# Moving gate weights out of the router and into the token sums of a fused attention and mixture-of-experts kernel

## The chip, the cores and the metric

One core of one Trainium2 chip runs the whole block as one program. The metric is the device time of an execution in microseconds (us). Smaller is better.

## The reference

Inputs are x (4 x 1024 tokens of 256), a context of 4 x 154 rows of 192, a key mask and two gates. With layernorm LN:

```
x = x + tanh(g_xattn) * Attention(LN(x), ctx, mask)   # 8 heads of 64
x = x + tanh(g_ffn)   * FFN(LN(x))
FFN(h): scores = sigmoid(h @ gate_w.T)                 # 32 experts in 8 groups of 4
        sc = scores + e_bias; keep the 4 groups with the largest sum of their top 2
        pick the top 6 of what is left; w = scores there / (their sum) * 2.5
        out = sum over the 6 of w * relu(h @ up_e.T)^2 @ down_e.T     # inner 128
            + relu(h @ up_sh.T)^2 @ down_sh.T                        # inner 512
```

## The kernel before

The 4096 tokens are 32 tiles of 128 (the partitions). Every engine runs a program written out by hand; semaphores order them. Helpers are called in loops over a slot T or a pair p, and the order of the calls in a slot is the engine's order.

**Maps.** PE makes keys and values of the context in 16 groups through a ring of seven PSUM banks; ACT saves the even groups, VectorE (DVE) the odd ones. In ACT's program the tanh of the gates stands ahead of all saves, and behind the loads of context and constants that ACT issues (L489 to L499). In DVE's, the constants (L701 to L708) stand ahead of all saves. SP loads weights, x and a transposed x.

**Attention.** In slot T of 35, PE does the scores of tile T (L1167), transposes the probabilities of tile T-2 (L1200), queries of T+2 (L1113), head outputs of T-2 (L1213) and the output projection of T-3 (L1223). DVE takes maxima (L751), inverts sums, normalises every other pair of tiles, adds the residual and takes its statistics. ACT makes exponentials and copies. The router works on blocks of four tiles, spread over slots: statistics to normed tiles in `norm_out` (T % 4 == 2), transposes and logits on PE (T % 4 == 3), `router_groups` and `router_select` (T % 4 == 0), `ranks` on PE and `router_slots` on DVE (T % 4 == 1). `router_slots` also makes a one-hot array `hot` and `picked`, its product with the scores (L913, L916); the weights are summed and scaled in instructions threaded through the next `norm_out` (L785 to L807).

**Rows.** POOL scatters each normed tile six times, once for each pick, to `routed_rows` in DRAM, at the place that the rank gives in its expert's region (L443). A row holds 256 values, six place keys (`R_ID`), six weights (`R_W`), six target rows (`R_TO`) and two more, 276 in all. Six scatters are issued in a slot from T = 11 on, each behind a wait on the other engines' progress (`slot_step`); the last 54 follow without such waits.

**Tables.** Counts of each expert give 224 tiles of 128 rows. SP writes a padding tile at each expert's end (32 DMAs of 138 KB), then loads rows.

**Expert pairs.** For p in 0 to 111: SP loads two tiles of rows to a ring of six pairs; PE does `expert_down` (L1428) of p-2, `expert_up` (L1413) of p and transposes (L1401) of p+2; ACT saves transposes, copies up weights (L640) and scales and saves the output of even pairs (L651); DVE does `relu_square` (L1038, L1040), `pick_rows` for two pairs (weights and target rows, L1024 to L1033), and scales and saves odd pairs (L1049). POOL scatters the outputs to `token_parts` (L479), into eight buffers in turn. Row tiles from pair 14 on wait for all of the scatters of `routed_rows`. In 28 of the pairs, PE also does a step of the shared expert (`SHARED_STEP`; L1299 up, L1309 down). From p = 51 on ACT loads the six parts of a token tile (768 KB) every 2.2 pairs (`PART_LOAD`), and DVE adds them in three steps in the three pairs from p + 3 (L1057; L1059, L1060; L1062).

**End.** Four shared down products and adds in turn on one bank, then the last four token tiles: two parts added by DVE, four by PE with an identity (L1455), the sum by DVE (L1093).

## Time and profile before

| | |
|---|---|
| median of 3 runs | 759.53 us (757.47 to 766.26) |
| profiled execution | 762.32 us, its span 760.5 us |
| mean granted TensorE clock | 0.989 |
| busy: PE, DVE, ACT, POOL | 705.1 (93%), 518.9 (68%), 454.1 (60%), 469.1 us (62%) |
| DRAM | 144.74 MB in 78238 packets, mean 190 GB/s |

Busy is the time in which an engine has an instruction in work; waits and drains do not count. A row of the timeline has the start in us from the span's start, the duration, engine, line, operation, tiles and shapes, and in brackets the idle time ahead of it with what ended it.

### The profile page before, as it was taken

Reading aid. Unit: us, or ns where it says so; the run is one execution under the profiler, and the core shown is the slowest. Engines: PE = TensorE matmul, PEld = TensorE weight load, DVE = VectorE, ACT = ScalarE, POOL = GpSimd, SP = SyncE. Lnnn points to the kernel's source line nnn. Section 1 sums busy time; section 2 is a strip of 40 time slices with the busy share of each in tenths; the row PEclk is TensorE's granted clock in tenths of the full one; section 3 lists DMA queues with packets and bytes.
Section 4 is the critical chain, followed back from the end, with each engine's and each line's share of the span. In section 5 each row is a group of like instructions: output and inputs, shape, how many; then the busy total and the mean of one; then the engine's idle time right before and its main releaser. Section 6 shows DMA issues by size and latency. Waiting matters only on the chain.

```text
span 760.5 us, 17775 instructions
## 1 busy us (share of the span) xinstructions
PE 705.1 (93%) x5416; PEld 600.7 (79%) x5416; DVE 518.9 (68%) x1783; ACT 454.1 (60%) x1299; POOL 469.1 (62%) x478
## 2 busy tenths in 40 slices
PE   7979898999999999989998999999998999999968
PEld 7768797888888888775674898988897788888756
DVE  0757578787878787876461556555567788888783
ACT  0257576778787878773515556566655666566620
POOL 1235442466666666577777477777775777777671
PEclk9999999999999999999999999999999999999998
DMA  9970000135222222354759866656689999999854
GB/s 311 376 227 1 1 3 1 54 105 190 89 96 93 91 91 91 110 189 158 275 176 303 227 212 194 207 169 185 211 262 290 327 325 351 316 369 315 261 208 153
DMA packets 78238, 144.74 MB, mean 190 GB/s; under 512 B 13750, under 2 KB 60097, under 8 KB 77120
## 3 DMA queue, kind: packets, MB, share of 16 engines
q1 hardware_dynamic: 51472, 67.46, 28.7%
q0 software_dynamic: 19968, 52.34, 18.8%
q10 hardware_dynamic: 6704, 23.80, 9.4%
q8 instruction: 45, 0.74, 0.4%
q14 instruction: 49, 0.40, 0.2%
HBM read 78.00 MB, written 69.73 MB: 194 GB/s over the span
## 4 chain that ended last, share of the span: by engine, by line
PE 46%; DVE 17%; DMA 9%; POOL 7%; issue 7%; ACT 6%; DVEq 6%; SPq 2%; ACTq 1%; POOLq 0%
PE ps L1428 8%; PE ps L1413 7%; POOL routed_rows L443 7%; DMA mid<-routed_rows 7%; PE ps L1401 4%; PE ps L1223 4%; PE ps L1213 4%; PE ps L1309 4%; ACT att L529 3%; PE ps L1167 3%; PE ps L1113 2%; PE ps L1200 2%; DMA gate_w<-in_gate_t 2%; DVEq L1076 2%; PE ps L1299 2%
## 5 line engine op out<-in xcount | busy, mean ns | idle before, releaser
L443 POOL DMA_INDIRECT routed_rows<-x_n,slots x120 | 119.9, 999 | 68.1 <-issue 31.6
L479 POOL DMA_INDIRECT token_parts<-hid,place x112 | 114.6, 1024 | 50.6 <-issue 26.2
L1428 PE MATMUL ps<-big,att 128*128 x448 | 118.8, 388 | 6.7 <-DVE picked L1049 3.2
L627 ACT ACTIVATE att<-ps 128x512 f32<-128x512 f32 x96 | 57.3, 597 | 97.4 <-PE ps L1401 96.2
L1413 PEld LDWEIGHTS ps<-att 128*128 128x128 f32 x768 | 100.8, 192 | 5.0
L1413 PE MATMUL ps<-att 128*128 128x128 f32 x768 | 101.2, 275 | 0.0
L1428 PEld LDWEIGHTS ps<-big,att 128*128 128x128 f32 x448 | 78.4, 190 | 27.0 <-issue 20.2
L529 ACT ACTIVATE att<-ps,nmax,rstd 128x154 f32<-128x154 f32 x176 | 82.0, 494 | 13.4 <-DVE nmax L756 13.2
L1213 PE MATMUL ps<-att,big 128*64 128x128 f32 x1024 | 70.3, 280 | 16.0 <-ACT att L546 11.3
L640 ACT ACTIVATE att<-big 128x256 f32 x224 | 80.1, 408 | 1.9 <-issue 1.2
L1213 PEld LDWEIGHTS ps<-att,big 128*64 128x64 f32 x1024 | 59.6, 138 | 23.5 <-ACT att L546 13.8
L1401 PE MATMUL ps<-cst,mid 128*128 128x128 f32 x448 | 67.9, 274 | 9.6 <-DMA mid<-routed_rows 9.4
L546 ACT ACTIVATE att<-ps 128x512 f32<-128x512 f32 (+1 forms) x96 | 48.4, 551 | 32.2 <-PE ps L1200 32.2
L751 DVE TENSOR_REDUCE nmax<-ps 128x3 f32<-128x462 f32 (+1 forms) x96 | 52.2, 572 | 20.0 <-PE ps L1167 20.0
L443 POOL DMA_INDIRECT routed_rows<-big,slots x48 | 49.6, 1032 | 22.0 <-issue 11.4
L1113 PE MATMUL ps<-big,hid 128*128 128x128 f32 x512 | 62.6, 275 | 0.0
L1401 PEld LDWEIGHTS ps<-cst,mid 128*128 128x128 f32 x448 | 52.1, 141 | 12.5 <-DMA mid<-routed_rows 9.9
L1038 DVE TENSOR_SCALAR hot<-ps 128x256 f32<-128x256 f32 x56 | 23.8, 425 | 54.6 <-PE ps L1401 53.0
L1223 PE MATMUL ps<-hid,big 128*128 128x256 f32 x256 | 61.0, 381 | 0.0
L1113 PEld LDWEIGHTS ps<-big,hid 128*128 128x128 f32 x512 | 59.7, 192 | 0.3 <-issue 0.3
L1223 PEld LDWEIGHTS ps<-hid,big 128*128 128x128 f32 x256 | 46.2, 190 | 5.8 <-issue 0.5
L529 ACT ACTIVATE big<-ps,nmax,rstd 128x154 f32<-128x154 f32 x80 | 37.3, 496 | 5.3 <-DVE nmax L756 5.3
(252 smaller groups left out, 1450.4 us busy)
## 6 DMA issues: line engine op xcount, KB each, us to landing
mid<-routed_rows SPq DMA_DIRECT2D x224, 138.0 KB
big<-token_parts ACTq DMA_DIRECT2D x19, 768.0 KB, 7.2
x_n<-token_parts ACTq DMA_DIRECT2D x9, 768.0 KB
routed_rows<-pad_row SPq DMA_DIRECT2D x1, 4416.0 KB
routed_rows<-pad_row SPq DMA_DIRECT2D x32, 138.0 KB
x_all<-in_x SPq DMA_DIRECT2D x4, 1024.0 KB, 12.9
big<-in_x_t SPq DMA_DIRECT2D x4, 1024.0 KB, 15.6
big<-in_w_moe SPq DMA_DIRECT2D x2, 2048.0 KB, 8.8
```

The source lines that it names most:

```text
L443: nc.gpsimd.indirect_dma_start(rows, bass.IndirectOffsetOnAxis(ap=slots[:, t, k:k + 1], axis=0), normed(t), None).then_inc(s_sca[t // TB % ...
L479: nc.gpsimd.indirect_dma_start(parts, bass.IndirectOffsetOnAxis(ap=place[:, p // 2 % 8, p % 2 * 2 + j:p % 2 * 2 + j + 1], axis=0), y_sb[p ...
L529: ins = A.activation(prob[T % 3][:, h * JP:h * JP + J], ps[:, q, i * J:(i + 1) * J], ACT.Exp, bias=nmax[:, T % 2, h:h + 1], scale=rstd1[:, ...
L627: A.activation(xt(p), ps[:, p % 2, :], ACT.Copy).then_inc(s_xts, 1)
L640: ins = A.activation(w_up[p % 2][:, j, :], w_exp[:, bass.ds(e, 1), 0:256].rearrange("p a n -> p (a n)"), ACT.Copy)
L751: V.tensor_reduce(nmax[:, T % 2, h:h + n], ps[:, q, 0:n * J].rearrange("p (a j) -> p a j", a=n), op=ALU.max, axis=AX_X, negate=True)
L1113: ins = M(ps[:, 6, m * P:(m + 1) * P], wq[:, c, m * P:(m + 1) * P], xt_in[:, T, c, :], start=c == 0, stop=c == KC - 1, skip_group_check=True)
L1213: ins = M(ps[h % 2 * DH:(h % 2 + 1) * DH, 7, h // 2 * P:(h // 2 + 1) * P], v_all[b][:, at:at + DH], prob_t[:, c * P:(c + 1) * P], start=c ...
L1223: ins = M(ps[:, 7, 0:D], att_t[:, m * P:(m + 1) * P], wo[:, m, :], start=m == 0, stop=m == MC - 1, skip_group_check=True)
L1401: ins = nc.tensor.transpose(ps[:, p % 2, j * 256 + c * P:j * 256 + (c + 1) * P], ring[:, p % 6, j, c * P:(c + 1) * P], ident)
L1413: ins = M(ps[:, 2 + p % 2, j * P:(j + 1) * P], w_up[p % 2][:, j, c * P:(c + 1) * P], xt(p)[:, j * 256 + c * P:j * 256 + (c + 1) * P], star ...
L1428: ins = M(ps[:, 6 + p % 2, j * D:(j + 1) * D], h_t[:, p % 2, j * P:(j + 1) * P], w_exp[:, bass.ds(e, 1), 256:512].rearrange("p a n -> p (a ...
```

## The change

1. Rows no longer carry weights (270 values). SP stores the router's scores of each block to DRAM and loads them all back ahead of row tile 14. In pairs 16 to 47 DVE finds each pick's expert from its place (a region is now 9 x 512 rows), marks it, picks the score and norms the weights to `w_tok`. `add_parts` becomes six multiply-adds. ACT and DVE save expert outputs unscaled; the wait for `pick_rows` goes from ACT's save to POOL's scatter.
2. Attention: `router_select` is split; the second part runs in T % 4 == 1 behind maxima and residual. `ranks` runs behind the head outputs, `router_slots` in T % 4 == 2 ahead of statistics and `norm_out`.
3. POOL's scatters start at slot 10, place k = 3; a memset (`pause`) follows each of the 51 behind the slots.
4. Start: SP loads the context first; tanh and constants move between the saves.
5. End: the last block's shared up steps move out of the pairs to behind them, on banks 0 to 3; down products alternate between two banks; the last tiles' parts are summed by DVE alone.

```diff
-REGION = N_TOK + P
+REGION = 9 << 9
+PAUSE = 320
-R_ID, R_W, R_TO, R_BASE, ROW = D, D + TOPK, D + 2 * TOPK, D + 3 * TOPK, D + 3 * TOPK + 2
+R_ID, R_TO, R_BASE, ROW = D, D + TOPK, D + 2 * TOPK, D + 2 * TOPK + 2
+WEIGH = {16 + 2 * i: 2 * i for i in range(NT // 2)}
+NORM_T = 8
-LATE = [(i, s) for i in range(FULL, NBLK) for s in range(8) if i >= GAP or s >= 4][:-TB]
+LATE = [(i, s) for i in range(FULL, NBLK) for s in range(8) if i >= GAP or s >= 4][:-2 * TB]
...
+            load_ctx(0)
             sp.dma_start(wk, w_k).then_inc(s_wk, 16)
             sp.dma_start(wv, w_v).then_inc(s_wv, 16)
+            load_ctx(2)
+            sp.dma_start(wq, w_q).then_inc(s_wq, 16)
             load_x(0)
-            sp.dma_start(wq, w_q).then_inc(s_wq, 16)
...
+            def store_scores(b):
+                sp.wait_ge(s_score, b + 1)
+                sp.dma_start(scores[:, b * TB * NE:(b + 1) * TB * NE], score[:].rearrange("p t e -> p (t e)")).then_inc(s_sst, 16)
...
                     sp.wait_ge(s_zf, 16 * (NE + 1))
+                    sp.wait_ge(s_sst, 16 * NBLK)
+                    sp.dma_start(old_rows[:, 0:NT * NE], scores).then_inc(s_sld, 16)
                 load_rows(p)
...
+            def pause():
+                if paused[0]:
+                    pool.wait_ge(s_pause, paused[0])
+                else:
+                    pool.wait_ge(s_xb, NT)
+                paused[0] += 1
+                nc.gpsimd.memset(bias_o[:].bitcast(BF16)[:, 0:PAUSE], 0.0).then_inc(s_pause, 1)
...
-            for T in range(11, NT + 2):
+            for T in range(10, NT + 2):
                 for k in range(TOPK):
                     slot_step(T, k)
-                    scatter((T - 11) * TOPK + k)
-            for i in range((NT + 2 - 11) * TOPK, NT * TOPK):
+                    if (T - 10) * TOPK + k >= 3:
+                        scatter((T - 10) * TOPK + k - 3)
+            for i in range((NT + 2 - 10) * TOPK - 3, NT * TOPK):
                 scatter(i)
+                pause()
...
                 pool.wait_ge(s_ey[p % 2], p // 2 + 1)
+                pool.wait_ge(s_pick, p // 2 + 1)
...
-            act.wait_ge(s_const, 16 * 6)
-            A.activation(tanh_g[:], gates[:], ACT.Tanh).then_inc(s_tanh, 1)
-            act.drain()
...
-                if g == 8:
+                if g == 6:
+                    act.wait_ge(s_const, 16 * 6)
+                    A.activation(tanh_g[:], gates[:], ACT.Tanh).then_inc(s_tanh, 1)
+                    act.drain()
+                if g == 12:
                     act.wait_ge(s_wo, 16)
...
-                act.wait_ge(s_pick, p // 2 + 1)
-                for j in range(2):
-                    ins = A.activation(y_sb[p % 8][:, j * D:(j + 1) * D], ps[:, 6, j * D:(j + 1) * D], ACT.Copy,
-                                       scale=pair_w[:, p // 2 % 8, j, 0:1])
-                ins.then_inc(s_ey[0], 1)
+                A.activation(y_sb[p % 8], ps[:, 6, :], ACT.Copy).then_inc(s_ey[0], 1)
...
-                if g == 3:
+                if g == 5:
                     stats(0)
                     stats(2)
                     norm_in_scale(0, 4)
+                if g == 7:
+                    constants()
...
+                if T % 4 == 1 and T >= 9:
+                    residual_add(T - 3)
+                    router_select()
...
-                    if T % 4 or T < 8:
+                    if T % 4 > 1 or T < 8:
                         residual_add(T - 3)
+                    if T % 4 == 2 and T >= 10:
+                        router_slots((T - 10) // 4)
                     residual_stats(T - 3)
-                if T % 4 == 1 and T >= 9:
-                    router_slots((T - 9) // 4)
...
-                    router_select((T - 8) // 4)
+                    router_top_groups()
...
+            def mark_experts(t):
+                V.tensor_tensor(hot, w_tok[:, t:t + 2, :].unsqueeze(3).broadcast_to([P, 2, TOPK, NE]),
+                                iota_e.unsqueeze(1).unsqueeze(1).broadcast_to([P, 2, TOPK, NE]), ALU.is_equal)
+            def pick_scores(t):
+                dve.drain()
+                V.tensor_tensor(hot, hot, score_t[:, t:t + 2, :].unsqueeze(2).broadcast_to([P, 2, TOPK, NE]), ALU.mult)
+                dve.drain()
+                V.tensor_reduce(w_tok[:, t:t + 2, :], hot, op=ALU.add, axis=AX_X)
+            def add_weighted(t, g, k):
+                return V.scalar_tensor_tensor(x_all[:, t, :], g[:, k, :], w_tok[:, t, k:k + 1], x_all[:, t, :], ALU.mult, ALU.add)
             def add_parts(t, step):
                 g = parts_sb[t % 3]
                 if step == 0:
                     dve.wait_ge(s_pl[t % 3], 16 * (t // 3 + 1))
-                    V.tensor_tensor(g[:, 0:3, :], g[:, 0:3, :], g[:, 3:6, :], ALU.add)
...
+                add_weighted(t, g, 2 * step)
+                dve.drain()
+                ins = add_weighted(t, g, 2 * step + 1)
...
+                for k in range(TOPK):
+                    if k == TOPK - 1 and t < NT - 1:
+                        add_late(t)
+                        dve.drain()
+                    ins = add_weighted(t, sums[:, t - NT + N_LAST, :, :], k)
+                    dve.drain()
+                ins.then_inc(s_fin, 1)
...
-                if T % 4 == 1 and T >= 9:
-                    ranks((T - 9) // 4)
                 if 2 <= T < NT + 2:
                     probs_t(T - 2, 1)
...
                     heads_out(T - 2)
+                if T % 4 == 1 and T >= 9:
+                    ranks((T - 9) // 4)
...
+            for s in range(4):
+                if s in (0, 2):
+                    pe.wait_ge((s_xts, s_eht)[s // 2], N_PAIRS)
+                up_late(LAST, s)
             for t in range(NT - TB, NT):
                 down_late(t)
-            for t in range(N_LAST):
-                pe.wait_ge(s_pl2[t], 16)
-                for k in range(2, TOPK):
-                    ins = M(ps[:, t, 0:D], ident, sums[:, t, k, :], start=k == 2, stop=k == TOPK - 1)
-                ins.then_inc(s_pp, 1)
```

## Rows read from the trace of the kernel before

**Rows 1.** Timeline of the head.
```profile
7.44 4.39 PE L1125 MATMUL ps<-mid,hid 128*128 128x308 f32 x16 [1.38 <-DMA mid<-in_ctx_t]
...
20.03 0.20 ACT L499 ACTIVATE tanh_g<-gates 128x2 f32<-128x2 f32 x1 [11.79 <-DMA gate_w<-in_gate_t]
...
20.80 2.89 PE L1134 MATMUL ps<-hid,mid 128*128 128x128 f32 x16 [3.61 <-ACT big L517]
...
41.02 0.50 PE L1157 MATMUL ps<-mask_bf,ones_bf 64*128 64x308 bf16 x3
```

**Rows 2.** Timeline of PE, slots 24 to 26.
```profile
262.51 1.33 PE L1167 MATMUL ps<-big 64*128 64x154 f32 x16
...
279.83 1.31 PE L1213 MATMUL ps<-att,big 128*64 128x128 f32 x18 [1.37 <-ACT att L546]
...
281.28 1.33 PE L1167 MATMUL ps<-big 64*128 64x154 f32 x16
```

**Rows 3.** Timeline of DVE: norm_out 0, maxima 25, norm_out 5, places of block 6.
```profile
97.71 0.17 DVE L782 TENSOR_SCALAR nwt<-mv 128x4 f32<-128x4 f32 x1
...
100.66 0.74 DVE L822 TENSOR_SCALAR x_n<-x_all,mv,rstd 128x256 f32<-128x256 f32 x2
...
274.56 0.58 DVE L751 TENSOR_REDUCE nmax<-ps 128x3 f32<-128x462 f32 x1
...
286.39 0.17 DVE L782 TENSOR_SCALAR nwt<-mv 128x4 f32<-128x4 f32 x1
...
290.92 1.50 DVE L822 TENSOR_SCALAR big<-x_all,mv,rstd 128x256 f32<-128x256 f32 x4
...
350.60 0.26 DVE L888 TENSOR_TENSOR key<-ps,cst 128x128 f32<-128x128 f32 x1
...
352.47 0.95 DVE L913 TENSOR_TENSOR hot<-key,best 128x768 f32<-128x768 f32 x1
```

**Rows 4.** Timeline of PE, pairs 14, 32 and 36.
```profile
449.71 0.60 PE L1401 MATMUL ps<-cst,mid 128*128 128x128 f32 x4
...
504.81 1.05 PE L1413 MATMUL ps<-att 128*128 128x128 f32 x8
...
515.61 1.05 PE L1413 MATMUL ps<-att 128*128 128x128 f32 x8
```

**Rows 5.** DVE's waits (total, times, longest) in 423:546, then in 563.56:719.06.
```profile
DVE hot L1038 <- PE ps L1401: 27.8, 23, 2.4
DVE x_n L1038 <- PE ps L1401: 16.2, 23, 1.6
...
DVE hot L1038 <- PE ps L1401: 6.5, 8, 1.8
DVE x_n L1038 <- PE ps L1401: 4.4, 5, 2.4
```

**Rows 6.** One window: length, busy of PE, PEld, DVE, ACT, POOL; clock, DMA, GB/s.
```profile
563.56:719.06 155.50, 146.74 (x930) 126.82 (x928) 128.97 (x364) 93.16 (x227) 111.62 (x106) 1.00 0.95 319
```

**Rows 7.** Timeline of POOL: a memset, first and last scatter behind the slots.
```profile
3.35 0.38 POOL L420 MEMSET run<- 128x352 bf16 x1
...
354.56 0.96 POOL L443 DMA_INDIRECT routed_rows<-big,slots  x1 [0.30 <-issue]
...
421.88 0.96 POOL L443 DMA_INDIRECT routed_rows<-att,slots  x1 [0.30 <-issue]
```

**Rows 8.** Timeline of DVE: old sums of a token tile, a multiply-add.
```profile
645.43 0.96 DVE L1057 TENSOR_TENSOR big<-big 128x768 f32<-128x768 f32 x1
...
647.90 0.41 DVE L1059 TENSOR_TENSOR big<-big 128x256 f32<-128x256 f32 x1
...
650.53 0.48 DVE L832 SCALAR_TENSOR_TENSOR x_all<-ps,tanh_g,x_all 128x256 f32<-128x256 f32 x1
```

**Rows 9.** Timeline of the end: a down product of PE, DVE's last add.
```profile
740.29 3.78 PE L1309 MATMUL ps<-w_shared,hid 128*128 128x256 f32 x8 [4.13 <-DVE x_all L832]
...
757.94 0.42 DVE L1093 TENSOR_TENSOR x_all<-ps,x_all 128x256 f32<-128x256 f32 x1 [0.47 <-PE ps L1455]
```

More of the change, by code:

```diff
@@ L66 @@
 DONE = [-(-((TOPK * P * t + NE * (P - 1)) // P) // 2) for t in SEG_END[:-1]]
+WEIGH = {16 + 2 * i: 2 * i for i in range(NT // 2)}
+NORM_T = 8
+assert N_TOK + P <= REGION == 9 << 9 and max(WEIGH) < 56 and all(9 * e * 57 >> 9 == (9 * e + 8) * 57 >> 9 == e for e in range(NE))
 assert (TOPK * P * EARLY - NE * (P - 1)) // P >= 2 * EARLY_PAIRS
@@ L306, in x2t_bank, with down_bank, up_bank @@
             return 5 if j == 0 else 6 if b < NBLK - 1 else 4
+        def down_bank(t):
+            return 4 if t >= NT - TB and t % 2 else 5
+        def up_bank(i, s):
+            return 4 if i < LAST else s
         def xt(p):
@@ L459, in slot_step @@
                     pool.wait_ge(s_pt, 3 * T - 3)
-            for T in range(11):
-                if T < 10:
-                    normalise(T)
+            for T in range(10):
+                normalise(T)
                 if T < 8:
@@ L486, in _ @@
             A = nc.scalar
-            for b in range(0, NB, 2):
-                for c in range(2):
-                    act.dma_start(ctx_w[:, c, b:b + 2, P:P + J],
-                                  ctx_t[:, c, b * J:(b + 2) * J].rearrange("p (b j) -> p b j", b=2)).then_inc(s_ctx[b // 2], 16)
             act.dma_start(gates[:, 0:1], g_xattn.partition_broadcast(P)).then_inc(s_const, 16)
@@ L699, in newton, with constants @@
                     dve.drain()
[L701 to L708 removed]
+            def constants():
+                dve.wait_ge(s_const, 16 * 6)
+                dve.wait_ge(s_tanh, 1)
+                dve.wait_ge(s_mrow, 16)
+                V.tensor_scalar(mask_bf[:].rearrange("p b j -> p (b j)"), mask_u8, -1.0, MASKED / DH, ALU.add, ALU.mult).then_inc(s_mask, 1)
+                V.tensor_copy(tri_bf[:], cst[:, C_TRI:C_TRI + P])
+                V.tensor_scalar(bias_o[:], bias_o[:], tanh_g[:, 0:1], None, ALU.mult)
+                dve.wait_ge(s_clr, 1)
+                V.memset(pad_row[:, R_BASE:R_BASE + 1], 1.0).then_inc(s_ready, 1)
             def stats(t):
@@ L779, in norm_out @@
                 a, half, tmp = [nwt[:, i, 0:TB] for i in range(3)]
-                r, w = normed_blk(max(b - 1, 0)), weight[:]
                 dve.drain()
@@ L899, in router_slots @@
                 dve.drain()
-                V.tensor_copy(normed_blk(b)[:, :, R_ID:R_ID + TOPK], best[:, :, 0:TOPK])
-                V.tensor_scalar(slots[:, TB * b:TB * b + TB, :], best[:, :, 0:TOPK], -1.0, None, ALU.add)
                 if TB * b + 3 in SEG_END:
@@ new lines, in norm_weights @@
+            def norm_weights(t):
+                w = w_tok[:, t:t + NORM_T, :]
+                dve.drain()
+                V.tensor_reduce(total[:], w, op=ALU.add, axis=AX_X)
+                dve.drain()
+                V.tensor_scalar(total[:], total[:], 1e-20, None, ALU.add)
+                dve.drain()
+                V.reciprocal(total[:], total[:])
+                dve.drain()
+                V.tensor_scalar(total[:], total[:], tanh_g[:, 1:2], ROUTED_SCALE, ALU.mult, ALU.mult)
+                dve.drain()
+                ins = V.tensor_tensor(w, w, total[:].unsqueeze(2).broadcast_to([P, NORM_T, TOPK]), ALU.mult)
+                if t + NORM_T == NT:
+                    ins.then_inc(s_wt, 1)
@@ L1056, in add_parts @@
                     dve.wait_ge(s_pl[t % 3], 16 * (t // 3 + 1))
-                    V.tensor_tensor(g[:, 0:3, :], g[:, 0:3, :], g[:, 3:6, :], ALU.add)
-                elif step == 1:
-                    V.tensor_tensor(g[:, 0, :], g[:, 0, :], g[:, 1, :], ALU.add)
-                    V.tensor_tensor(x_all[:, t, :], x_all[:, t, :], g[:, 2, :], ALU.add)
-                else:
-                    V.tensor_tensor(x_all[:, t, :], x_all[:, t, :], g[:, 0, :], ALU.add).then_inc(s_fin, 1)
+                add_weighted(t, g, 2 * step)
+                dve.drain()
+                ins = add_weighted(t, g, 2 * step + 1)
+                if step == 2:
+                    ins.then_inc(s_fin, 1)
             for p in range(N_PAIRS + 2):
@@ L1081, in _ @@
                         dve.drain()
-            for t in range(NT - TB, NT):
-                add_late(t)
-            dve.drain()
             for t in range(NT - N_LAST, NT):
-                g = sums[:, t - NT + N_LAST, :, :]
+                if t == NT - 1:
+                    add_late(t)
+                    dve.drain()
                 dve.wait_ge(s_pl2[t - NT + N_LAST], 16)
-                V.tensor_tensor(g[:, 0, :], g[:, 0, :], g[:, 1, :], ALU.add)
-                dve.drain()
-                V.tensor_tensor(x_all[:, t, :], x_all[:, t, :], g[:, 0, :], ALU.add)
-                dve.drain()
-                dve.wait_ge(s_pp, t - NT + N_LAST + 1)
-                V.tensor_tensor(x_all[:, t, :], ps[:, t % 4, 0:D], x_all[:, t, :], ALU.add).then_inc(s_fin, 1)
+                for k in range(TOPK):
+                    if k == TOPK - 1 and t < NT - 1:
+                        add_late(t)
+                        dve.drain()
+                    ins = add_weighted(t, sums[:, t - NT + N_LAST, :, :], k)
+                    dve.drain()
+                ins.then_inc(s_fin, 1)
         @block.tensor
```

144 lines of the change are left out of this document (72 added, 72 removed).

## The prediction, made before the result was known

> **What bounds the kernel now.** I read the stages first, then in each one the wait that ends last. Of the span of 760.5 us, the first 41.5 us set up, an attention loop of 32 slots ends near 356, shared work and tables run to 414, 112 pairs of expert tiles to 734, and the end takes the rest. In all of them TensorE is nearly always busy, but what breaks its row differs.
>
> Head: PE waits 3.61 us for a copy that ACT makes at 20.3, because ACT's first instruction, the tanh, waits for the last constant, to 20.03 [rows 1].
>
> Attention: slots 24 and 25 together take 18.8 us (262.51 to 281.28). PE's own work is 8.4 in each, and 0.3 for the ranks in slot 25, which holds a wait of 1.37 at the head outputs, for a copy by ACT [rows 2]. So slot 25 takes 10.4. Its scores were ready near 272.2, but VectorE took their first maximum at 274.56 [rows 3], behind the expert selection. ACT's exponentials, and the copies behind them, start late by those 2.3 us.
>
> Expert pairs: four pairs take 10.80 us while PE alone is the limit (504.81 to 515.61) [rows 4]: 2.19 a pair, 1.7 for a shared step that is in one of the four, some 0.3 for loading registers. From about pair 54, when finished tokens are also summed, VectorE has little left: it waited 44.0 us in 423 to 546, and only 10.9 in the 155.5 us from the up product of pair 54 to that of pair 107 [rows 5], though PE idles there too for want of rows. DMA is busy 95% of that stretch [rows 6].
>
> **The change, part by part**, in us of the profiled execution (762.3 with 1.8 outside its span; the median of the runs, 759.5, stands 2.8 lower, so I add the sum to that).
>
> *Head.* ACT's context loads go to SP's queue ahead of the rest, and tanh moves behind the save of map group 4. PE then has no reason for the 3.61 wait; VectorE's constants move behind group 7, so its first copies, held back as well, come early: the 16 matmuls behind the wait span 2.89, about 1.1 over their work, and the next groups stall again, together some 1.5 (an estimate). The start at 7.44 waited 1.38 for the context [rows 1]; it is now first on its queue but the key weights come third, bounds 0 and 1.38, I take 0.5. Tile loads follow later on SP; I estimate 13 to 15 us against their use in VectorE's group 5. Sum -5.5, bounds -3 to -6.5. If x were late, its statistics would only delay group 7, which PE needs 12 us later.
>
> *Attention.* Selection is cut: top groups stay in the slot T % 4 == 0, the 2.5 us from the comparison to the selected mask move behind the maxima of the next slot, ranks behind that slot's head outputs. VectorE's work in T % 4 == 0, from the first maximum about 10 us, falls by 2.5 and below 8.4, so the maxima come when the scores do. The slot of 10.4 should take 8.7: 1.65 each, six slots (9 to 29): -9.9. Against it: places move into T % 4 == 2, ahead of the normalisation. From key to places is 1.87 us (350.60 to 352.47), about 1.95 with the copy of target rows; the weights that were threaded through norm_out go, 4.53 us with them (286.39 to 290.92) and 2.95 without (97.71 to 100.66) [rows 3]. Net 0.35 later for the normed tiles, which PE's next transposes already wait for: six times, +2.1. Slot 33 gains a wait for the mask, +0.5. Sum -7.3; bounds -4 and -10. Slots then sit at PE's own work, so nothing beyond this is to be had. The removed one-hot product, multiply and sum (three of 0.95 a block) save nothing more, since they lay beside PE. Storing scores costs eight small DMAs on SP, whose waits all come before the weight loads behind them are due: 0.
>
> *Tables to the first pair.* The places of the last block are free of weights, but PE is still in its shared products when they come. 0.
>
> *Pauses.* Scatters begin three earlier, so 51 instead of 54 are left when the slots end: at 1.27 each from 354.56, they would end at 419.3 rather than 422.8. But each of the 51 is now followed by a memset of 320 bf16 on POOL. The nearest row is the memset of 352 bf16, 0.38 us [rows 7]. The gap of 0.30 ahead of every scatter may hide most of it (0.05), or be paid twice (0.65). I take 0.38: POOL ends at 438.7. Queued behind are the output scatters, some 9 us later than now, and on SP the wait for all scatters before row tile 14, then the 512 KB of scores. PE transposes pair 14 at 449.71 [rows 4]; landing (about 3), issue and the loads (about 6.5) end at 448. It fits by 1.5 us. Up to 0.41 a pause costs nothing, 0.65 costs 12. POOL, 9 us later, is just inside the eight output buffers: +1.
>
> *Early pairs, weights.* VectorE makes the token weights in pairs 16 to 47: per two tiles a comparison, a product and a sum of 384 elements. 768 take 0.95 [rows 3], so 384 about 0.55, 1.63 with two drains; times 16 is 26.1; four norms of 1.35, 5.4; the expert numbers, 1.6; less 16 times 0.06 for a smaller pick: 32.1. Idle was 44.0 in 46 pairs, 30.6 in these 32. VectorE is full: +1.5. With POOL's 1: +2.5, bounds -2 (rows sooner in emptier queues) and +14 (pauses exposed).
>
> *Late pairs.* A tile's sum was one add of 768 at 0.96 and three of 256 at 0.41 to 0.42, with drains and overlap 2.37. It becomes six multiply-adds of 256 with a per-partition scalar, each behind a drain. The trace has that form only from PSUM, 0.48 [rows 8]; adds cost the same from either memory, so six times (0.48 + 0.07) is 3.3, +0.93. If the scalar were free, six times 0.49 gives +0.6. VectorE worked 155.5 - 11.7 = 143.8 us in the stretch (its waits for PE are 10.9, two others 0.8). 24 tiles add 22.3, the smaller pick takes 1.6: 164.5, and with 1 us of leftover idle the stretch takes 165.5: +10. With a free scalar 158: +3. This also eats what four shared up products (6.9 us of PE), moved behind the loop, would have given.
>
> This is the point where the Trainium skill speaks against the change. The rows show three times the elements at 0.96 against 0.41, so 0.27 us of the smaller cost follow the elements and 0.15 come with each instruction. The Trainium skill (VectorE: DVE Perf Modes, the section on the TRN2 errata) says that operations on SBUF pay a fixed latency per instruction and wants tiles of 512 elements or more; its formula for fp32 adds, (N + 151) / 0.96, gives an estimate of 2.54 us for six against 2.23 for the old four, +0.3 a tile before drains and scalar. By that alone the stretch would be about 3 us shorter than mine. The trace agrees with the formula to 2%.
>
> *End.* Before, the last tiles went down, add, down on one bank, one down product taking 3.78, twice its usual 1.9, from 740.29 to the last add at 757.94 [rows 9]. Now PE does four ups after pair 111 (6.9), the squares end 1.3 later, and down products alternate banks. VectorE finishes its queue 2 us later than it did (four dearer tiles less idle), then does seven operations of 0.55 for each of four tiles: 15.4 where it was 18.7 (the last pair's sums ended at 739.7). PE holds the first back 0.7. Sum -0.7, bounds -3 and +5 (downs at half clock).
>
> Sum: -5.5 - 7.3 + 2.5 + 10 - 0.7 = -1.0. That is 758.5.
>
> **Rivals.** *Late pairs are not VectorE's (faster).* For: VectorE had 10.9 us to spare, PE loses 6.9 us of work, and the price of the multiply-add is not seen from SBUF. Against: of those 10.9 most fall where PE itself waited for rows. With +1 to +3 for the stretch, the head and attention stay whole: 749.5.
>
> *Pauses exposed (slower).* In POOL's tail, at a pause of 0.65 a scatter, SP's wait before tile 14 holds every later row: +12, so 770. It decides from 0.41. For: gaps between scatters are never under 0.30, so another instruction may add its own. Against: that memset of 0.38 was itself followed by the next after 0.32.
>
> *The end at half clock.* PE idles more beside a full VectorE and meets the last downs at 3.8 instead of 1.9: +5, 763.
>
> *The stall moves.* The change does not do what it says: places and normalisation fill T % 4 == 2 (about 9.5 us for 8.4), and the stall returns one slot later. Then attention gives 1 instead of 7.3: 765.
>
> **How the numbers follow.** Forecast 0.42 (own range 752 to 765), late pairs cheap 0.32, pauses 0.14, half clock 0.05, stall moves 0.07. A measurement of this kernel cannot tell 1% from no change. Faster by over 1% (under 751.9) takes nearly all of the second and a little of the first: 0.36. Slower by over 1% (over 767.1) takes pauses, half of the last and the forecast's upper tail: 0.22. Within: 0.42. The range leaves one in ten outside at each end: 746 to 771.
>
> **What would show it.** Head: first scores near 35.5 instead of 41.02. Attention: T % 4 == 1 slots at 8.7, and T % 4 == 3 slots 0.3 longer. Pauses: spacing of the last 51 scatters 1.65, and no PE wait for rows at pair 14. Late pairs: VectorE without waits, 3.1 us a pair, PE idle. The multiply-add at 0.48. I am wrong if PE's cadence past pair 54 stays 2.9 or less, or if tile 14 is waited for.

## The result and the profile after

The changed kernel takes 769.8 us (median of 20 runs, 766.95 to 774.77) where the kernel before takes 760.8 on the same chip (756.01 to 767.39): a ratio of 1.0121, 95% interval 1.0100 to 1.0142. It is slower, by 1.2%. The prediction was 758.5. Medians and ratios, here and in the experiments, leave out the few executions that ran far longer than the rest (1005.5 us once in experiment 1, 1404.0 once in experiment 2). The profiled execution took 769.17 us, its span 767.4, at a mean granted clock of 0.982.

Cut at the same events, the two spans differ like this (starts of the scores of slots 0 and 3, of the up products of pairs 0, 54 and 107, and the span's end; all from TensorE's timeline):

| stretch | before | after | difference | predicted |
|---|---|---|---|---|
| to the first scores | 41.23 | 36.17 | -5.06 | -5.5 (head) |
| slots 0 to 2 | 21.02 | 23.99 | +2.97 | 0 |
| slot 3 to pair 0 | 354.05 | 346.48 | -7.57 | -7.3 |
| pairs 0 to 54 | 147.26 | 146.44 | -0.82 | +2.5 |
| pairs 54 to 107 | 155.50 | 170.94 | +15.44 | +10 |
| pair 107 to the end | 41.46 | 43.36 | +1.90 | -0.7 |
| span | 760.52 | 767.38 | +6.86 | -1.0 |

The stretch of pairs 54 to 107, one window as in [rows 6]: length, busy time of PE, PEld, DVE, ACT and POOL, clock, DMA share and rate.

```profile
553.08:724.02 170.94, 143.72 (x913) 126.28 (x912) 145.15 (x411) 83.39 (x196) 109.24 (x109) 0.98 0.90 292
```

Beside [rows 6] DVE has 16 us more to do in 47 more instructions, PE 3 less, and DMA is less busy. What PE waits for in that window (total, times, longest), and what DVE does (busy us, mean ns, idle ahead of it):

```profile
PE ps L1492 <- DVE spare L1065: 9.6, 6, 1.9
PE ps L1492 <- DVE hid L1065: 7.5, 7, 1.9
PE ps L1492 <- DVE att L1057: 3.7, 8, 0.6
PE ps L1492 <- DVE big L1065: 3.2, 2, 2.1
PE ps L1465 <- DMA mid<-routed_rows: 2.9, 1, 2.9
```

```profile
L1105 DVE SCALAR_TENSOR_TENSOR x_all<-big,w_tok,x_all 128x256 f32<-128x256 f32 x96 | 46.3, 482 | 4.8
L1105 DVE SCALAR_TENSOR_TENSOR x_all<-x_n,w_tok,x_all 128x256 f32<-128x256 f32 x46 | 22.1, 481 | 2.3
```

The down product (L1492) waits for VectorE's copy of an output out of its bank (L1065) or for its square (L1057), 24.0 us in all; in the kernel before its waits for VectorE are 0.9, and those for rows 6.3. What keeps VectorE so long stands in the second fence: 142 multiply-adds of 0.48 us. How they follow each other, in VectorE's timeline of two pairs:

```profile
599.71 1.03 DVE L1105 SCALAR_TENSOR_TENSOR x_all<-x_n,w_tok,x_all 128x256 f32<-128x256 f32 x2
600.83 1.04 DVE L1105 SCALAR_TENSOR_TENSOR x_all<-big,w_tok,x_all 128x256 f32<-128x256 f32 x2
601.95 0.42 DVE L1055 TENSOR_SCALAR spare<-ps 128x256 f32<-128x256 f32 x1
602.46 0.42 DVE L1057 SCALAR_TENSOR_TENSOR att<-ps,spare 128x256 f32<-128x256 f32 x1
...
603.63 0.16 DVE L1050 TENSOR_TENSOR place<-pair_to,to_spill 128x4 uint32<-128x4 f32 x1
603.71 1.04 DVE L1105 SCALAR_TENSOR_TENSOR x_all<-big,w_tok,x_all 128x256 f32<-128x256 f32 x2
604.82 0.42 DVE L1055 TENSOR_SCALAR x_n<-ps 128x256 f32<-128x256 f32 x1
```

There is no gap: a step of two, each behind a drain, takes 1.12 to 1.14 us from start to start (600.83 less 599.71, 601.95 less 600.83), three steps 3.4 a tile where the prediction reads 2.37 for the old sum.

The attention loop, against [rows 2] and [rows 3]: PE's slots 24 to 26, and VectorE's maximum of slot 25.

```profile
254.86 1.33 PE L1228 MATMUL ps<-big 64*128 64x154 f32 x16
...
263.23 1.33 PE L1228 MATMUL ps<-big,x_n 64*128 64x154 f32 x16
...
269.25 2.22 PE L1274 MATMUL ps<-att,big 128*64 128x128 f32 x32
271.40 0.23 PE L1321 MATMUL ps<-sel,tri_bf 128*128 128x128 bf16 x1
...
271.92 1.33 PE L1228 MATMUL ps<-big 64*128 64x154 f32 x16
```

```profile
264.62 0.64 DVE L798 TENSOR_REDUCE nmax<-ps 128x3 f32<-128x462 f32 x1 [0.49 <-PE ps L1228]
```

Slot 25 takes 8.69 us and has no wait at the head outputs (L1274); the maximum now waits for the scores, not they for it. One slot in four (T % 4 == 3) pays for it. PE's timeline in slot 19:

```profile
210.08 1.39 PE L1299 MATMUL ps<-cst,x_n 128*128 128x128 f32 x8 [0.99 <-DVE x_n L853]
```

The transposes of the normed tiles wait 0.99 us for the normalisation.

The pauses, in POOL's timeline against [rows 7]:

```profile
343.71 0.96 POOL L489 DMA_INDIRECT routed_rows<-big,slots  x1 [0.30 <-issue]
344.67 0.38 POOL L483 MEMSET bias_o<- 128x320 bf16 x1
345.22 0.97 POOL L489 DMA_INDIRECT routed_rows<-big,slots  x1 [0.17 <-issue]
346.18 0.39 POOL L483 MEMSET bias_o<- 128x320 bf16 x1
```

A scatter with its pause takes 1.51 us (345.22 less 343.71), 0.25 more than the 1.26 without. The last scatter ends at 421.64, before the up product of pair 14 at 444.09, and nobody waits for it.

The end, VectorE's last tiles, against [rows 9]:

```profile
747.66 3.87 DVE L1105 SCALAR_TENSOR_TENSOR x_all<-big,w_tok,x_all 128x256 f32<-128x256 f32 x7
752.32 0.48 DVE L863 SCALAR_TENSOR_TENSOR x_all<-ps,tanh_g,x_all 128x256 f32<-128x256 f32 x1 [0.79 <-PE ps L1373]
...
761.94 3.28 DVE L1105 SCALAR_TENSOR_TENSOR x_all<-big,w_tok,x_all 128x256 f32<-128x256 f32 x6
```

From 747.66 to 765.22 there is one gap of 0.79: this is one chain of drained multiply-adds.

### The profile page after: what moved, and what is told of

The parts are those of the page before. It is cut to its first block, busy times and chain, and to the rows that moved or that the text cites. A ratio compares the mean times of both kernels' runs of the same rounds, so it can differ in the third digit from the quotient of the medians.

```text
span 767.4 us, 17935 instructions
## 1 busy us (share of the span) xinstructions
PE 699.0 (91%) x5384; PEld 599.4 (78%) x5384; DVE 547.4 (71%) x1859; ACT 441.6 (58%) x1243; POOL 484.1 (63%) x529
## 4 chain that ended last, share of the span: by engine, by line
PE 51%; DVE 24%; DVEq 11%; issue 7%; ACT 3%; DMA 2%; SPq 2%; POOL 0%; ACTq 0%; POOLq 0%
DVE x_all L1105 8%; PE ps L1274 6%; PE ps L1284 6%; PE ps L1174 5%; DVEq L1112 4%; PE ps L1339 4%; PE ps L1492 4%; PE ps L1228 4%; PE ps L1261 3%; PE ps L1477 3%; PE ps L1351 3%; DMA mid<-routed_rows 2%; PE ps L1195 2%; PE ps L1465 2%; PE ps L1373 2%
## 5 line engine op out<-in xcount | busy, mean ns | idle before, releaser
L1492 PE MATMUL ps<-big,att 128*128 x448 | 121.8, 395 | 30.6 <-DVE spare L1065 13.1
L527 POOL DMA_INDIRECT token_parts<-hid,place x112 | 112.7, 1006 | 46.5 <-issue 25.4
L1492 PEld LDWEIGHTS ps<-big,att 128*128 128x128 f32 x448 | 79.2, 193 | 50.6 <-issue 43.4
L1274 PE MATMUL ps<-att,big 128*64 128x128 f32 x1024 | 69.6, 281 | 6.3 <-DVE x_all L816 4.1
L527 POOL DMA_INDIRECT token_parts<-spare,place x56 | 56.5, 1010 | 29.7 <-issue 14.5
L1105 DVE SCALAR_TENSOR_TENSOR x_all<-big,w_tok,x_all 128x256 f32<-128x256 f32 x138 | 66.6, 483 | 7.8
L1274 PEld LDWEIGHTS ps<-att,big 128*64 128x64 f32 x1024 | 60.1, 138 | 12.8 <-DVE x_all L816 5.5
L489 POOL DMA_INDIRECT routed_rows<-big,slots x48 | 48.3, 1005 | 23.1 <-issue 14.6
```

Source lines behind the costliest of these rows:

```text
L489: nc.gpsimd.indirect_dma_start(rows, bass.IndirectOffsetOnAxis(ap=slots[:, t, k:k + 1], axis=0), normed(t), None).then_inc(s_sca[t // TB % ...
L527: nc.gpsimd.indirect_dma_start(parts, bass.IndirectOffsetOnAxis(ap=place[:, p // 2 % 8, p % 2 * 2 + j:p % 2 * 2 + j + 1], axis=0), y_sb[p ...
L1105: return V.scalar_tensor_tensor(x_all[:, t, :], g[:, k, :], w_tok[:, t, k:k + 1], x_all[:, t, :], ALU.mult, ALU.add)
L1274: ins = M(ps[h % 2 * DH:(h % 2 + 1) * DH, 7, h // 2 * P:(h // 2 + 1) * P], v_all[b][:, at:at + DH], prob_t[:, c * P:(c + 1) * P], start=c ...
L1492: ins = M(ps[:, 6 + p % 2, j * D:(j + 1) * D], h_t[:, p % 2, j * P:(j + 1) * P], w_exp[:, bass.ds(e, 1), 256:512].rearrange("p a n -> p (a ...
```

## The experiments

These numbers of each kernel are compared throughout. "Idle" is the sum of the gaps of over 0.12 us between VectorE's rows in the stretch from pair 54 to 107, "work" the stretch less that (instructions and their drains). Each ratio is to runs of the kernel before that were made beside that experiment, on the same chip; their medians were 762.2 to 762.8 us (760.8 beside the changed kernel), so medians of different rows can differ by some 2 us for that alone, and kernels are compared by ratio. The other columns come from one trace each.

| kernel | median, us | ratio to before, 95% | pair 0 starts | pairs 0 to 54 | 54 to 107: length, idle, work | 107 to end |
|---|---|---|---|---|---|---|
| before | 760.8 | 1 | 416.3 | 147.3 | 155.5, 12.0, 143.5 | 41.5 |
| changed | 769.8 | 1.0121 (1.0100 to 1.0142) | 406.6 | 146.4 | 170.9, 5.1, 165.8 | 43.4 |
| 1: no pauses | 775.9 | 1.0204 (1.0096 to 1.0313) | 407.4 | 147.5 | 168.7, 2.5, 166.2 | 44.8 |
| 2: plain sums | 750.6 | 0.9873 (0.9828 to 0.9918) | 406.4 | 148.1 | 149.8, 7.4, 142.3 | 41.9 |
| 3: late ups in pairs | 768.6 | 1.0109 (1.0079 to 1.0140) | 406.7 | 147.6 | 171.2, 5.4, 165.9 | 42.6 |
| 4: head only | 758.4 | 0.9957 (0.9928 to 0.9985) | 413.4 | 147.8 | 154.3, 10.8, 143.4 | 40.8 |
| 5: mixed sums | 754.5 | 0.9917 (0.9878 to 0.9956) | 405.2 | 148.1 | 155.6, 7.1, 148.5 | 42.0 |
| 6: ranks split | 767.6 | 1.0061 (1.0034 to 1.0088) | 402.2 | 148.3 | 170.3, 4.3, 166.0 | 44.8 |
| 7: no token weights | 768.9 | 1.0077 (1.0041 to 1.0112) | 409.7 | 145.6 | 168.4, 2.0, 166.4 | 45.0 |
| 8: mixed, split, end | 749.0 | 0.9812 (0.9773 to 0.9852) | 401.9 | 148.8 | 154.8, 6.4, 148.5 | 41.0 |
| 9: before, half parts | 756.5 | 0.9925 (0.9891 to 0.9959) | 419.1 | 148.0 | 148.3, 4.3, 144.0 | 39.6 |
| 10: changed, half parts | 772.2 | 1.0136 (1.0070 to 1.0202) | 409.9 | 148.9 | 168.7, 2.5, 166.2 | 43.7 |

Five kernels have the changed kernel's code in the late pairs: the changed one and experiments 1, 3 (but for the up products), 6 and 7. They took 168.4 to 171.2 us with 2.0 to 5.4 of it idle. What an experiment moves there by less than that says little.

**1. No pauses.** The changed kernel without them:

```diff
             for i in range((NT + 2 - 10) * TOPK - 3, NT * TOPK):
                 scatter(i)
-                pause()
```

> The changed kernel without the 141 clears of GpSimd between the tail scatters. Theory (VectorE's multiply-adds in the late pairs made the loss): the tail ends some 35 us sooner, nobody waits for it, and the time stays within 2 us of the changed kernel, 768 to 771. Rival (the pauses are exposed): the time falls by 6 us or more, to 764 or less, and the first 30 pairs get shorter.

The scatters ended at 408.9 instead of 421.6, 13 us sooner and not 35 (51 pauses stand there, not the 141 that the expectation counts), and the pairs to 54 were 1.1 us longer, not shorter. The median of three runs, 775.9, is above the 768 to 771 that was expected, and its interval is wide; it holds the changed kernel's ratio. Nothing speaks for a price of the pauses: the rival falls.

**2. Plain sums.** The 24 tiles that are summed in the pairs are added as before the change, so their gate weights are left out:

```diff
-                add_weighted(t, g, 2 * step)
-                dve.drain()
-                ins = add_weighted(t, g, 2 * step + 1)
...
+                    V.tensor_tensor(g[:, 0:3, :], g[:, 0:3, :], g[:, 3:6, :], ALU.add)
+                elif step == 1:
+                    V.tensor_tensor(g[:, 0, :], g[:, 0, :], g[:, 1, :], ALU.add)
+                    V.tensor_tensor(x_all[:, t, :], x_all[:, t, :], g[:, 2, :], ALU.add)
+                else:
+                    V.tensor_tensor(x_all[:, t, :], x_all[:, t, :], g[:, 0, :], ALU.add).then_inc(s_fin, 1)
```

> The changed kernel with the sums of the 24 tiles that go in the pairs written as before, without the gate weights (their part of the output is therefore left unweighted); all else as changed. Theory: VectorE gets 24 x 1.05 = 25 us of work back, TensorE or the output slots bound the late pairs, which fall from 171 to 152 to 158 us, and the time is 752 to 758, below the kernel before. Rival (the late pairs are long because of transfers or GpSimd's scatters, which now run in another order): the late pairs stay at 165 or more and the time at 764 or more.

```profile
554.49:704.24 149.75, 139.48 (x914) 123.87 (x912) 127.75 (x364) 83.55 (x196) 111.59 (x107) 1.00 0.97 331
```

The late pairs fell by 21.2 us, to 149.8, and the kernel to 750.6. VectorE's work fell by 23.5 us (25 expected). This one edit turns a loss of 1.2% into a gain of 1.3%; transfers and scatters were left as they are, and DMA moved more per us than in any other run. The multiply-adds, with the drain behind each, are the cause of the loss. (TensorE's granted clock is 0.98 of full speed in the changed kernel's stretch and 1.00 in this one. That is 3.4 us at most, 2% of 171, of the 21.2.)

**3. Late up products in the pairs.** The last block's four shared up products go back among the pairs (the four calls behind the loop, on PE and ACT, and their banks are taken out as well):

```diff
-LATE = [(i, s) for i in range(FULL, NBLK) for s in range(8) if i >= GAP or s >= 4][:-2 * TB]
+LATE = [(i, s) for i in range(FULL, NBLK) for s in range(8) if i >= GAP or s >= 4][:-TB]
```

> The changed kernel with the last block's four shared up products back in the pairs, as before the change, instead of behind them. Theory (VectorE bounds the pairs and the end alike): TensorE has the room, the late pairs grow by 0 to 2 us, the end loses 0.8 to 2, the time stays within 2 us of 770. Rival (the up products behind the pairs are what made the end 1.9 us longer, and they were worth nothing in the pairs): the time falls by 3 us or more, to 767 or less.

6.9 us of TensorE's work came back into the stretch and it grew by 0.3; the end lost 0.8, less than the ends of kernels with the same code there differ (43.4 to 45.0). The ratio hardly differs from the changed kernel's. TensorE has room there, as the theory says, and moving that work out of the pairs shows no gain beside a full VectorE.

**4. The head alone**, on the kernel before: the context first on SP's queue, ahead of the key weights, tile loads behind the query weights, tanh at group 6, and on VectorE:

```diff
-                if g == 3:
+                if g == 5:
                     stats(0)
...
+                if g == 7:
+                    constants()
```

> The kernel before, with nothing of the change but its first loads, the tanh, the constants and the first statistics where the change has them. Theory: the first scores start 5 us sooner (36.2 for 41.2) and all that follows moves with them, so the time falls by 4 to 5.5 us, to 755 to 757 where the kernel before has 760.8. Rival (the work that the head gives up fills slots 1 and 2, which were 3.0 us longer in the changed kernel): the first pair starts only 2 to 3 us sooner and the time falls by 2 to 3.

Scores started at 36.0, 5.2 sooner, but slot 3 only 3.6 sooner and pair 0 only 2.9; the median fell by 4.0 us against the runs beside it, and the ratio is 0.43% under 1 (3.3 us, 1.1 to 5.5). By its size that is between theory and rival, and the interval holds both. The rival's reason can be tested on the traces. Here are slots 0 to 2, one window each as in [rows 6], with the old head in the kernel before and in experiment 9, then with the new one in experiments 3 and 4 and in the changed kernel:

```profile
41.23:62.25 21.02, 14.42 (x151) 12.39 (x149) 14.09 (x52) 14.29 (x55) 8.60 (x8) 1.00 0.50 155
42.33:64.97 22.64, 17.04 (x151) 14.82 (x149) 14.35 (x54) 14.24 (x55) 8.59 (x8) 0.85 0.40 126
36.27:57.28 21.01, 14.41 (x151) 12.38 (x148) 14.07 (x52) 14.28 (x55) 8.60 (x8) 1.00 0.92 246
36.03:58.67 22.64, 17.13 (x151) 14.91 (x148) 14.36 (x54) 14.24 (x55) 8.59 (x8) 0.85 0.77 237
36.17:60.16 23.99, 18.81 (x151) 16.43 (x149) 14.63 (x54) 14.23 (x55) 8.59 (x8) 0.79 0.77 218
```

The number third from the end is TensorE's mean granted clock; it has two levels, 2.4 GHz (1.00) and 1.2 GHz (0.50). At full clock these slots take 21.0 us with either head, and at 0.85 22.64 with either; VectorE is busy for 14.1 to 14.6 us and ACT for 14.2 to 14.3 in all five. The changed kernel's extra 3.0 us came with some 10 us at 1.2 GHz, and not with work that the head gave up: the rival's reason is wrong. Just ahead of the first fall, in 39.30 to 42.70, TensorE was busy for 0.78 us; in experiment 3 it was busy for as little in the same stretch, and its clock stayed full. The lower clock shows in these slots in seven of the ten traces with the new head and in one of the two with the old, too few to say that the head brings it on.

**5. Mixed sums.** The same multiply-adds in the same order on each tile. In even pairs the first of a step stands among the operations that pick the places, in odd pairs all first ones stand ahead of one drain and all second ones behind it:

```diff
                 V.tensor_reduce(pair_to[:], pick[:], op=ALU.add, axis=AX_X)
+                for t, step in firsts:
+                    add_half(t, step, 0)
                 dve.drain()
                 V.tensor_tensor(place[:, q % 8, :], pair_to[:], to_spill[:], ALU.add).then_inc(s_pick, 1)
+                for t, step in seconds:
+                    add_half(t, step, 1)
```

> The changed kernel with the same multiply-adds, but the first of each step is put among the operations that pick the places (even pairs) or beside that of another tile, and the drains that stood behind each of the two are left to those that stand there anyway. Theory (VectorE's time, of it a good part the drains, sets the late pairs): each step falls from 1.14 us to 0.75 to 0.85, 72 steps by 0.3 to 0.4 = 21 to 28 us of VectorE, the late pairs go from 171 to 153 to 160 us and the time to 752 to 760. Rival (the multiply-adds themselves at 0.48 cost the time, drains lie beside them): the late pairs fall by less than 5 us and the time stays at 765 or more.

VectorE's timeline, to be held against the one of the changed kernel above:

```profile
600.57 1.83 DVE L1109 SCALAR_TENSOR_TENSOR x_all<-big,w_tok,x_all 128x256 f32<-128x256 f32 x4
603.13 0.42 DVE L1059 TENSOR_SCALAR spare<-ps 128x256 f32<-128x256 f32 x1 [0.74 <-PE ps L1476]
```

```profile
553.23:708.82 155.59, 142.94 (x913) 126.76 (x912) 136.47 (x411) 82.60 (x194) 108.24 (x107) 0.98 0.95 317
```

Two steps take 1.83 us from start to end where they took 2.16 (599.71 to 601.87), and then VectorE waits for TensorE. That had waited 1.80 us for rows until 598.43, and from 599.7 to 603.1 its granted clock was half (eight up products took 1.92 us there, 1.05 elsewhere). Busy time fell by 8.7 us with the same 411 instructions, because two that overlap count once; work fell by 17.3 us, about 0.24 a step, less than the 0.3 to 0.4 that was expected. The late pairs and the time came out inside the forecast, 155.6 and 754.5: with the weights in the sums, and faster than before.

**6. Ranks split.** One operation of the ranks' work stays ahead of the normalisation, since it frees the bank; the rest goes behind it:

```diff
                     if T % 4 == 2 and T >= 10:
-                        router_slots((T - 10) // 4)
+                        read_ranks((T - 10) // 4)
                     residual_stats(T - 3)
...
                     norm_out((T - 6) // 4)
+                if T % 4 == 2 and T >= 10:
+                    router_slots((T - 10) // 4)
```

> The changed kernel, with only the one operation that reads the ranks out of the bank ahead of the normalisation in every fourth slot, and the rest of the ranks' work behind it. Theory (the normed tiles come late in slots T mod 4 = 3, since the whole of the ranks' work now stands ahead of them): each of the six slots falls by 0.4 to 0.9 us and the first pair starts 2 to 5 us sooner, the time is 765 to 768. Rival (the next wait stands right behind it): those slots fall by less than 0.3 each and the time stays.

PE's waits between slots 11 and 31 of the changed kernel, then of this one (total, times, longest):

```profile
PE ps L1299 <- DVE x_n L853: 2.5, 3, 1.0
PE ps L1274 <- ACT att L590: 1.6, 1, 1.6
PE ps L1299 <- DVE big L853: 1.4, 2, 0.9
```

```profile
PE ps L1279 <- ACT att L590: 1.6, 1, 1.6
```

The wait is gone, and slots 11, 15, 19, 23 and 27 fell from 55.5 us to 50.0, 1.1 each: more than the wait itself and more than expected. Slot 31 starts 8.3 us sooner than in the changed kernel, 1.8 of which are there at slot 3 already. Pair 0 starts only 4.5 sooner:

```profile
399.30 1.09 PE L1470 MATMUL ps<-cst,mid 128*128 128x128 f32 x4 [5.50 <-DMA mid<-routed_rows]
```

PE waits 5.50 us for the first rows, where the changed kernel has 1.88. So 3.6 us of the gain end there, and TensorE's granted clock is half from 396.5 to 406.8, where the changed kernel has it full; the first 16 pairs take 1.7 us longer. The ratio falls from 1.0121 to 1.0061, some 4.6 us, and the two intervals do not overlap.

**7. No token weights.** A constant stands in place of each token's gate weights, and the work that makes them is left out:

```diff
-                if p == min(WEIGH):
-                    experts_of_tokens()
...
+                    V.memset(w_tok[:], 0.25).then_inc(s_wt, 1)
```

> The changed kernel with the pairs' work on the tokens' weights left out: VectorE writes one constant in their place, so that the sums carry a wrong weight; all else as changed. Theory (that work lies almost wholly in VectorE's idle time): pairs 16 to 48 fall from 89.05 us by 0.5 to 1.5 and the time by as much. Rival (it costs what it takes, some 30 us of VectorE's work over 40 pairs, and delays what follows): pairs 16 to 54 fall by 4 us or more.

VectorE's waits in pairs 16 to 48, of the changed kernel and of this one:

```profile
DVE spare L1055 <- PE ps L1465: 1.7, 3, 0.7
```

```profile
DVE spare L1055 <- PE ps L1460: 18.6, 16, 2.4
DVE x_n L1055 <- PE ps L1460: 10.2, 14, 1.7
```

28.8 us of waits become 1.7 by that work, and the 32 pairs go from 86.58 to 89.05. It is 27 us of work for 2.5 of time. That is between theory and rival. Of the total no change is shown: the ratio, 1.0077, is 0.44% lower, and the intervals overlap.

**8. All three.** Mixed sums, split ranks, and at the end each tile's seven operations start three behind those of the tile ahead of it, two or three tiles between one pair of drains:

```diff
+            for slot in range(3 * (N_LAST - 1) + TOPK + 1):
+                for i in range(N_LAST):
+                    t, k = NT - N_LAST + i, slot - 3 * i
...
+                dve.drain()
```

> The changed kernel with the mixed sums of the run before (754.5), the ranks' work behind the normalisation, and the last four tiles' sums run two at a time, three steps apart, instead of one after the other. Theory: 754.5, less 2 to 4 for the slots, less 1 to 3 for the end, 748 to 752, which is faster than either kernel by over 1%. Rival (the end is bound by the last tile's load and its seven steps, and the slots by the next wait): 753 to 755.

749.0 us, 1.9% under the kernel before (1.5 to 2.3) in the runs beside it, and by the two ratios 3% under the changed kernel. It beats both. Its end, in VectorE's timeline, now has a wait for parts of one of the last tiles, which the order of the sums alone does not remove:

```profile
739.32 0.48 DVE L863 SCALAR_TENSOR_TENSOR x_all<-ps,tanh_g,x_all 128x256 f32<-128x256 f32 x1 [1.88 <-DMA big<-token_parts]
```

**9 and 10. Half the parts**, on the kernel before and on the changed one. What was open was the idle time: why 5.1 us of it were left under a full load. Only three of a tile's six parts are loaded, so half of each sum reads what lies in the buffer:

```diff
-                act.dma_start(parts_sb[t % 3].rearrange("p k d -> p (k d)"), part_tiles[t]).then_inc(s_pl[t % 3], 16)
+                act.dma_start(parts_sb[t % 3][:, 0:3, :].rearrange("p k d -> p (k d)"), part_tiles[t][:, 0:3 * D]).then_inc(s_pl[t % 3], 16)
```

> The kernel before, loading only the first half of each tile's six parts in the pairs (24 loads of 384 KB in place of 768 KB; the other half of the sums reads what lies in the buffer). Theory (of the late pairs' 12.0 us in which VectorE did nothing, some 6.5 came from row loads that land late behind the parts' traffic, and idle time of that kind can't take up more work): TensorE's waits for rows fall from 6.5 us to under 2.5, VectorE's idle time in the late pairs stays below 10, the late pairs go from 155.5 to 149 to 153. Rival (the row loads are late for another reason, or the late pairs have room elsewhere): TensorE's waits for rows stay over 5 us and the late pairs within 1 us of 155.5.

> The changed kernel with the same halved loads. Theory (VectorE's steps bound the late pairs, transfers only through some 3 to 5 us of idle time): the late pairs fall from 171 by 2 to 5 us only, VectorE's idle time there from 5.1 to under 3, the time is 765 to 768. Rival (contention of the transfers slows VectorE or TensorE themselves): the late pairs fall by 8 us or more and the time to 762 or less.

```profile
567.11:715.45 148.34, 144.51 (x929) 126.50 (x928) 129.03 (x364) 93.50 (x227) 111.84 (x106) 1.00 0.88 273
```

```profile
558.76:727.46 168.70, 143.43 (x913) 126.42 (x912) 145.35 (x411) 83.51 (x196) 109.16 (x109) 0.98 0.79 241
```

In the kernel before TensorE no longer waited for rows, VectorE's idle time fell from 12.0 to 4.3, and the stretch by 7.2 us, to 148.3, a little under the forecast. (Experiment 4, with full loads and the same code there, took 154.3 with 10.8 idle, so the fall is beyond such differences.) VectorE's work moved by 0.5 and 0.4 us, so lighter transfers don't make it faster. In the changed kernel the stretch fell by 2.2, and its idle time from 5.1 to 2.5. That is as forecast but shows nothing, since experiments 1 and 7 with full loads have 168.7 and 168.4 us with 2.5 and 2.0 idle. The total of 10, 772.2, missed its 765 to 768: pair 0 started 3.2 us late, ahead of all that was edited. Row loads that land late behind the parts stop PE, and with it VectorE; before the change that was most of VectorE's idle time. In the changed kernel little of it is left: TensorE waits 0.3 to 3.3 us for rows in the five kernels with full loads.

## Why the prediction was wrong

The mechanism of the likeliest case was right and the sign of the result was not. It was forecast that VectorE would set the late pairs, with TensorE idle, and it did; of the rivals, cheap late pairs (749.5) and exposed pauses (770) are both refuted, though the measured time lies beside the second. It is outside the forecast's own 752 to 765, and inside the 746 to 771 of all cases together. In the span the misses are +3.4 in the head, -0.3 in the attention, -3.3 in the early pairs, +5.4 in the late ones and +2.6 in the end, together +7.9 on the -1.0 of the sum. (The medians stand 9.0 apart, the two profiled spans 6.9.)

**Late pairs, +10 forecast, +15.4 measured.** This is the step that failed, and the largest of the misses: with this term at +10 and all others as measured, the span would have grown by 1.5 us in place of 6.9. Its price of work was nearly right: 22.3 more for the tiles less 1.6 for the pick made 20.7, and 22.3 was measured (165.8 less 143.5). The multiply-add took 0.482 us as priced, with 0.09 for its drain where 0.07 was assumed. What failed is "with 1 us of leftover idle": 5.1 were left. VectorE's idle time was treated as room to be filled, all but 1 us of 11.7. The prediction itself says of those waits that most fall where TensorE waited for rows, and used that only against the rival. In this trace 2.9 us went to one late row load, and 1.4 are short gaps that no other engine ended. 22.3 of work less 6.9 of idle time taken up is the 15.4. How much idle time stays is not fixed: the five kernels with this code left 2.0 to 5.4, on 165.8 to 166.4 of work. So the term was too small by 2.9 to 5.7 us, of which 1.3 to 1.9 is work and the rest idle time. The range had 158 to 165.5 for this stretch, so its upper side was not covered. The granted clock is the lesser part of it: 0.98 here for 1.00 before, and experiments 5 and 8, with one code in these pairs and the clock at 0.98 and 1.00, are 0.8 us apart.

The Trainium skill (VectorE: DVE Perf Modes, the section on the TRN2 errata) gives (N + 151) / 0.96 for an fp32 add, 0.42 us for 256 elements; the adds of experiment 2 take 0.414 to 0.419 and agree, and the multiply-add with its scalar from memory takes 0.06 more. The rule of the Trainium skill in the same section, that short operations pay a fixed part each, spoke against the change, with an estimate of +0.3 a tile. Measured are +1.0 (3.4 for 2.37), as scalar and drains come on top. The prediction's "about 3 us shorter than mine" does not come out of its own numbers: with a free scalar it has 158 for 165.5, which is 7.5 shorter.

**Head, -5.5 forecast.** The mechanism held: -5.1 at the first scores, and experiment 3, at full clock, still has 5.0 of it at slot 3 (57.28 for 62.25). In the changed kernel slots 1 and 2 took back 3.0, and experiment 4 shows the cause: TensorE's granted clock, at 1.2 GHz for some 10 us there. The prediction priced the clock at the end only and nowhere else. It is no sure cost of this change, since kernels with the same code to that point have from none to 10 us of it; what sets it off stays open.

**Attention, -7.3 forecast, -7.6 measured.** The six slots T % 4 == 1 fell from 62.7 us together to 52.0, 1.8 each (1.65 forecast). Slots T % 4 == 3 grew by 0.6 (0.35 forecast), since the transposes waited for the normed tiles, and experiment 6 shows that this was avoidable: with one operation of the ranks' work ahead of the normalisation instead of all they fall by 1.1. The wait for the mask in slot 33 came, 1.1 us (0.5 forecast).

**Pauses and early pairs, +2.5 forecast, -0.8 measured.** A pause added 0.25 of its 0.38 us, under the 0.41 from which it was to count, and PE did not wait for rows at pair 14. The first 16 pairs got 1.6 us shorter, 41.9 for 43.5, both at full clock; what shortened them is not shown. (The other kernels with that code took 42.9 to 44.3, with 3 to 5.5 us of it at half clock.) The weights cost 2.5 us by experiment 7 (1.5 forecast), but pairs 16 to 48 of the kernel before took 1.7 us more than those of experiment 7, so beside it only 0.8 shows.

**End, -0.7 forecast, +1.9 measured.** VectorE came to the last four tiles with a longer queue: seven multiply-adds stand in the row from 747.66, five of them those of tile 28, so the tiles of the pairs kept it until about 748.7. Then it did 28 drained operations of 0.57. The prediction let VectorE finish its queue 2 us later than before, counted from pair 107, and it was 4.0 later (748.7 less 724.0, against 739.7 less 719.1); the last four tiles took 16.5 where 15.4 was forecast. With a shorter queue (experiments 2 and 5) the end takes 41.9 and 42.0. The half-clock rival did not happen: the last down products took 1.8 to 2.0 each.

## What to carry to other kernels

Before filling an engine's idle time, split it by cause (a test with half the traffic shows how much of it comes from late transfers), and don't count on filling it all: of 12.0 us, 2.0 to 5.4 stayed under a full load. Before a few microseconds are given a cause, look at the granted clock of that stretch, and at other kernels with the same code there. When one long operation is broken into a chain of short dependent ones, the drains are a sixth of its price; put the links among other work on the same engine before judging the idea, as the same multiply-adds gave +1.2% in one order and -0.8% in the other. A step moved ahead of something that another engine waits for should be cut down to the one operation that must be there.

## What the runs showed of the hardware

A memset of 320 bf16 on GpSimd between two indirect DMAs took 0.38 us but spaced them only 0.25 further apart: the gap ahead of a scatter shrank from 0.30 to 0.17, and the memset followed the scatter with none.

Four multiply-adds with a drain behind each took 2.16 us from the first start to the last end; two independent ones, a drain, and the two that depend on them took 1.83.

With 14% less moved per us (DMA share 0.88 for 0.95, 273 for 319 GB/s), waits for row loads disappeared. At 0.95 to 0.97 (five kernels) the row loads were late six to ten times in 53 pairs, at 0.89 to 0.92 (five others, slowed by VectorE) once or twice.

The same work took TensorE's slots 0 to 2 21.0 us at a granted clock of 1.00, 22.4 to 23.0 at 0.85 and 24.0 at 0.79 (in one kernel, at 0.92, 21.1). In experiment 6 TensorE waited 5.50 us until 399.30, and its clock was at 1.2 GHz from 396.5 to 406.8. But a stretch in which TensorE was busy for 0.78 of 3.40 us was followed by the lower clock in the changed kernel and not in experiment 3.
